# Two cond blocks on one core: layer 1's normalized y transposed in 64-row tiles, two at a time, with every order and bank chosen anew

## The reference

```python
# layer 0 (8 heads of 32)
xn = ln(x); q = softmax(xn@Wq+bq, per head); k = softmax(xn@Wk+bk, over tokens); v = xn@Wv+bv
y  = q @ (k^T v)                                  # per head, 32x32 states
hh = ln(y)*(1+scale)+shift;  x = x + silu(hh) @ W_out + b_out
# layer 1 (16 heads of 16)
xn = ln(x); att = softmax(q k^T over m);  y = att @ v
h  = ln(y)*(1+scale)+shift;  x = x + silu(h) @ out_w + out_b
```

## Time and profile before

| | |
|---|---|
| median of 3 runs | 822.89 us (822.42 to 824.58) |
| profiled execution: span | 824.9 us, 27262 instructions |
| mean granted TensorE clock | 0.989 |
| busy: PE, DVE, ACT, POOL | 797.7, 735.6, 704.5, 688.7 us |
| PE matrix products | 9407 |

### The profile page before, as it was taken

One profiled execution on the slowest core, in us unless ns is written; L12 is line 12 of the kernel. 1 busy time (PEld: TensorE's weight loads), 2 busy tenths in 40 slices (PEclk: granted clock), 3 DMA queues, 4 the chain that ended last, 5 costly groups with the idle time before them and its releaser, 6 DMA issues.

```text
span 824.9 us, 27262 instructions
## 1 busy us (share of the span) xinstructions
PE 797.7 (97%) x9407; PEld 572.0 (69%) x9407; DVE 735.6 (89%) x1488; ACT 704.5 (85%) x1658; POOL 688.7 (83%) x1021
## 2 busy tenths in 40 slices
PE   7998999999999999999999999999999999999995
PEld 3575776777777777677777777777777777666643
DVE  6899999998989999989898889989898989898962
ACT  2366678999898998898898998889989999999995
POOL 8579899999878999789898999888889987896423
PEclk9899999999999999999999999999999999999998
DMA  7522355354344443334545543353454433444411
GB/s 184 153 40 67 96 140 133 81 119 112 86 108 109 105 126 102 98 90 98 122 107 136 121 98 84 84 134 106 110 122 109 109 88 80 99 104 128 116 34 39
DMA packets 149276, 86.11 MB, mean 104 GB/s; under 512 B 87404, under 2 KB 141802, under 8 KB 149130
## 3 DMA queue, kind: packets, MB, share of 16 engines
q1 hardware_dynamic: 149140, 84.36, 42.4%
HBM read 39.64 MB, written 25.80 MB: 79 GB/s over the span
## 4 chain that ended last, share of the span: by engine, by line
PE 41%; issue 12%; POOL 9%; DVE 9%; DMA 2%; SPq 1%; ACT 1%; POOLq 0%; DVEq 0%; ACTq 0%
PE banks L708 11%; PE banks L861 7%; PE banks L716 5%; PE banks L835 4%; PE banks L848 4%; PE banks L723 3%; DVE NM L1308 3%; PE banks L738 2%; PE banks L787 2%; PE banks L871 2%; DVE st L1199 1%; POOL YN L2015 1%; POOL rs L2011 1%; POOL ZHL L2036 1%; POOL SH L2088 1%
## 5 line engine op out<-in xcount | busy, mean ns | idle before, releaser
L1308 DVE TENSOR_REDUCE NM<-banks 128x4 f32<-128x1024 f32 x256 | 306.4, 1212 | 25.1 <-PE banks L835 24.0
L1807 ACT ACTIVATE wraw<-banks 128x1024 f32<-128x1024 f32 x154 | 155.9, 1034 | 8.0 <-PE banks L848 7.3
L2011 POOL TENSOR_TENSOR rs<-ve,nhalf 128x2 f32<-128x2 f32 x128 | 89.7, 703 | 31.6 <-ACT ve L1682 31.4
L1807 ACT ACTIVATE PX<-banks 128x1024 f32<-128x1024 f32 x102 | 103.5, 1035 | 8.6 <-PE banks L848 7.3
L2088 POOL TENSOR_TENSOR SH<-ST,SH 128x512 f16<-128x512 f32 x64 | 74.4, 1164 | 31.4 <-ACT SH L1771 31.4
L708 PE MATMUL banks<-wo,SH 128*128 128x256 f16 x768 | 94.9, 274 | 4.5 <-POOL SH L2088 4.4
L708 PE MATMUL banks<-wv,ZT 128*128 128x256 f16 x768 | 93.5, 273 | 1.4 <-DVE wv L1404 0.5
L835 PE MATMUL banks<-SK,SQ 51*128 51x256 f16 x1024 | 92.5, 272 | 0.8 <-ACT wemb L1815 0.3
L848 PE MATMUL banks<-SQ,SK 53*128 53x256 f16 x1024 | 90.6, 271 | 2.1 <-DVE NM L1308 1.0
L2036 POOL TENSOR_TENSOR ZHL<-Z,ZHL 128x256 f16<-128x256 f32 x128 | 87.5, 704 | 2.6
L861 PE MATMUL banks<-wraw,V 128*32 128x256 f32 x1232 | 87.2, 385 | 0.8 <-DVE NM L1308 0.8
(11 more groups left out here) (186 smaller groups left out, 1879.5 us busy)
## 6 DMA issues: line engine op xcount, KB each, us to landing
scr<-AB SPq DMA_DIRECT2D x64, 256.0 KB, 2.6
X<-in_x_dram SPq DMA_DIRECT2D x32, 256.0 KB, 2.8
SK<-scr SPq DMA_DIRECT2D x64, 128.0 KB, 2.9
SQ<-scr SPq DMA_DIRECT2D x64, 128.0 KB, 2.7
out_dram<-wemb SPq DMA_DIRECT2D x32, 256.0 KB, 2.5
SK<-scr SPq DMA_DIRECT2D x64, 64.0 KB, 2.9
SQ<-scr SPq DMA_DIRECT2D x64, 64.0 KB, 2.7
wemb<-in_L_cond_W_emb_dram SPq DMA_DIRECT2D x1, 1024.0 KB, 5.5
```

What stands on the lines that cost most here:

```text
L1308: V.tensor_reduce(NMe[:, c, :, 2 * g:2 * g + 2], banks[:, n:n + 2, :].rearrange("p a (h m) -> p a h m", m=T), AX.X, ALU.max, negate=True). ...
L1807: A.activation(px(v % 5), banks[:, n:n + 2, :].rearrange("p a n -> p (a n)"), ACT.Exp, scale=r_uu).then_inc(S["exp"])
L2011: G.tensor_tensor(rs[:, b % 2, l, :], ve[:, b % 2, l, :], nhalf[:, :], ALU.pow).then_inc(S[f"r{l}"])
```

## The change

`y1T` is no longer 4 transposes of 128 rows into one bank but 8 of 64 rows: each 128x128 block is turned as its lower and its upper 64 tokens, the lower into bank n and the upper into bank n+1, so that the two lie in different halves of the array. The moving operand, a piece of the identity, has 64 columns in place of 128, the stationary one 64x128. `th_of` reads layer 1's result over the two banks in runs of 64 elements and writes TH and HH as before (they stay contiguous). `gy1T` now needs two free banks, its first always 0, 2, 4 or 6.

```diff
+            def half_transposes(n, src):
+                for a in range(2):
+                    for f in range(2):
+                        for h in range(2):
+                            r = slice(HALF * h, HALF * h + HALF)
+                            m = PE.transpose(banks[:, n + h, f * P + a * HALF:f * P + a * HALF + HALF], src[r, a, f * P:(f + 1) * P],
+                                             ident[r, r])
+                return m
...
             def y1T(b):
                 e.wait_ge(S["yn1"], b + 1)
                 clear(e, "gy1T", b)
-                transposes(home("gy1T", b), YN[:, 1]).then_inc(S["y1T"])
+                half_transposes(home("gy1T", b), YN[:, 1]).then_inc(S["y1T"])
...
+            def turned(M, l, k):
+                return M[:, l, k, :].rearrange("p (a h j) -> p a h j", a=2, h=2) if l else M[:, l, k, :]
+
+            def of_turned(l, n, k):
+                if l == 0:
+                    return bank(n)[:, k, :]
+                return banks[:, n:n + 2, k * P:(k + 1) * P].rearrange("p h (a j) -> p a h j", a=2)
...
                 for k in range(2):
-                    A.activation(TH[:, l, k, :], bank(n)[:, k, :], ACT.Tanh, bias=hB[:, l, k, b:b + 1],
+                    A.activation(turned(TH, l, k), of_turned(l, n, k), ACT.Tanh, bias=hB[:, l, k, b:b + 1],
                                  scale=hA[:, l, k, b:b + 1])
                 for k in range(2):
-                    i = A.activation(HH[:, l, k, :], bank(n)[:, k, :], ACT.Identity, bias=fB[:, l, k, b:b + 1],
+                    i = A.activation(turned(HH, l, k), of_turned(l, n, k), ACT.Identity, bias=fB[:, l, k, b:b + 1],
                                      scale=fA[:, l, k, b:b + 1])
...
-    "gy1T": "71477300023554175724706543174653",
+    "gy1T": "22066264220466242404400406466600",
...
     "gy1T": (
-        "max:29 at:10 th0:9 exp:39 exp:47 exp:55 yt:31 exp:71 exp:79 exp:88 exp:95 yt:51 exp:110 max:132 "
+        "exp:16 Y0:9+at:10 max:46 max:53 max:61 exp:55 exp:64 exp:72 max:91 exp:88 max:109 exp:104 max:124 max:131 "
...
```

```diff
-            ld_m(); ld_w0(); x_in(0); x_in(1); ld_r(); ld_o0(); ld_c(); x_in(2); fd(); mbd0(); ld_f0(); z0T(0)
+            ld_m(); x_in(0); ld_w0(); mbd0(); ld_c(); x_in(1); fd(); ld_o0(); ld_r(); am(0); z0T(0); x_in(2); ld_f0()
```

More of the change, by code:

```diff
@@ L49 @@
[L49 to L67, removed]
@@ L91 @@
-    "go1": "77002057550012516235333440150322",
+    "gt_o0": "2",
+    "gbb0": "3",
+    "grow3": "4",
+    "ga_o0": "0",
+    "gcnd": "5",
+    "gbb1": "2",
+    "gk0": "14351504245220412017350771421607",
+    "gq0": "35223303754635105141241226740026",
+    "gfx0": "0",
+    "gkt": "11202545635546425571015676470564",
+    "gv0": "32466043371555444206274751561017",
+    "gqt": "21036120433375627000653471627452",
+    "gfm0": "0",
+    "gat": "10422543136026235740066601443662",
+    "gt_f0": "0",
@@ new lines @@
+    "gy0": "15411335220304445510026303622433",
+    "ga_f0": "0",
+    "gt_w1": "0",
+    "gy0T": "16740040625603506043370057055262",
+    "ga_w1": "0",
+    "gbb2": "1",
+    "go0": "63325724226635250043231133456224",
+    "grw": "3",
+    "gcol": "1",
+    "gt_b": "1",
+    "ga_b": "1",
+    "gfx1": "5",
+    "gk1": "00346633620523611774600256661352",
+    "gfm1": "0",
+    "gt_o1": "4",
+    "gq1": "24447740777543446542202644773223",
+    "gv1": "75275474474666446454757157617531",
+    "gt_f1": "1",
@@ new lines, in _ @@
+            rows(7, 5); pv(5, 6); pv(5, 7); v1p(8); q0(13); rows(7, 6); cols(6, 0); ty(5, 1); v0(13); cols(6, 1)
+            cols(6, 2); ktT(13); o1(4); qtT(12); rows(7, 7); cols(6, 3); cols(6, 4); o0(10); k1p(9); q1p(9)
+            rows(8, 0); pv(6, 0); pv(6, 1); cols(6, 5); rows(8, 1); rows(8, 2); pv(6, 2); pv(6, 3); pv(6, 4); pv(6, 5)
+            cols(6, 6); rows(8, 3); cols(6, 7); y0T(11); v1p(9); y0(12); rows(8, 4); y1T(5); pv(6, 6); att(13)
+            pv(6, 7); k0(14); cols(7, 0); rows(8, 5); qtT(13); q0(14); ty(6, 0); ty(6, 1); cols(7, 1); rows(8, 6)
@@ new lines, in _ @@
+            o1(5); ktT(14); k1p(10); o0(11); cols(7, 2); rows(8, 7); cols(7, 3); q1p(10); v0(14); cols(7, 4)
+            rows(9, 0); cols(7, 5); pv(7, 0); pv(7, 1); pv(7, 2); pv(7, 3); cols(7, 6); rows(9, 1); rows(9, 2)
+            pv(7, 4); pv(7, 5); rows(9, 3); cols(7, 7); y0(13); rows(9, 4); y1T(6); pv(7, 6); pv(7, 7); att(14)
+            ty(7, 0); y0T(12); k0(15); rows(9, 5); cols(8, 0); ty(7, 1); q0(15); v1p(10); cols(8, 1); cols(8, 2)
+            rows(9, 6); o1(6); v0(15); cols(8, 3); cols(8, 4); rows(9, 7); k1p(11); ktT(15); o0(12); qtT(14); q1p(11)
@@ new lines, in _ @@
+            cols(14, 5); rows(16, 1); pv(14, 0); pv(14, 1); pv(14, 2); pv(14, 3); rows(16, 2); cols(14, 6)
+            rows(16, 3); pv(14, 4); pv(14, 5); y1T(13); cols(14, 7); y0(20); ktT(21); ty(14, 0); y0T(19); v0(22)
+            k0(22); rows(16, 4); pv(14, 6); pv(14, 7); cols(15, 0); rows(16, 5); cols(15, 1); q0(22); cols(15, 2)
+            rows(16, 6); ty(14, 1); k1p(18); v1p(17); ktT(22); cols(15, 3); rows(16, 7); cols(15, 4); q1p(18); o1(13)
+            qtT(21); o0(19); rows(17, 0); cols(15, 5); rows(17, 1); pv(15, 0); pv(15, 1); att(21); pv(15, 2)
@@ new lines, in _ @@
+            o0(24); qtT(26); ktT(27); rows(22, 0); cols(20, 4); rows(22, 1); q1p(23); v1p(22); cols(20, 5)
+            rows(22, 2); pv(20, 0); pv(20, 1); pv(20, 2); pv(20, 3); rows(22, 3); rows(22, 4); cols(20, 6); y0(26)
+            y1T(19); rows(22, 5); y0T(25); ty(20, 0); k0(28); pv(20, 4); pv(20, 5); rows(22, 6); cols(20, 7)
+            cols(21, 0); q0(28); att(27); pv(20, 6); pv(20, 7); rows(22, 7); cols(21, 1); q1p(24); ty(20, 1); v0(28)
+            k1p(24); o1(19); cols(21, 2); rows(23, 0); cols(21, 3); v1p(23); ktT(28); qtT(27); o0(25); cols(21, 4)
@@ new lines, in _ @@
+            cols(21, 5); rows(23, 1); pv(21, 0); pv(21, 1); pv(21, 2); cols(21, 6); rows(23, 2); cols(21, 7)
+            pv(21, 3); pv(21, 4); pv(21, 5); att(28); rows(23, 3); rows(23, 4); y1T(20); y0(27); v0(29); pv(21, 6)
+            pv(21, 7); cols(22, 0); rows(23, 5); rows(23, 6); ty(21, 0); y0T(26); k0(29); qtT(28); cols(22, 1)
+            rows(23, 7); q0(29); ty(21, 1); v1p(24); o1(20); cols(22, 2); cols(22, 3); o0(26); cols(22, 4)
+            rows(24, 0); ktT(29); k1p(25); q1p(25); rows(24, 1); rows(24, 2); cols(22, 5); pv(22, 0); pv(22, 1)
@@ new lines, in _ @@
+            y0T(29); ty(24, 0); rows(26, 6); rows(26, 7); v1p(27); cols(25, 0); qtT(31); ty(24, 1); cols(25, 1)
+            cols(25, 2); k1p(28); o1(23); q1p(28); rows(27, 0); rows(27, 1); cols(25, 3); o0(29); pv(25, 0)
+            cols(25, 4); rows(27, 2); cols(25, 5); pv(25, 1); pv(25, 2); cols(25, 6); rows(27, 3); pv(25, 3)
+            pv(25, 4); pv(25, 5); cols(25, 7); rows(27, 4); y1T(24); y0(31); rows(27, 5); ty(25, 0); y0T(30)
+            pv(25, 6); pv(25, 7); rows(27, 6); cols(26, 0); v1p(28); ty(25, 1); cols(26, 1); rows(27, 7); cols(26, 2)
@@ new lines, in _ @@
+            pv(28, 7); cols(29, 0); cols(29, 1); rows(30, 7); ty(28, 1); v1p(31); cols(29, 2); cols(29, 3); o1(27)
+            cols(29, 4); rows(31, 0); pv(29, 0); pv(29, 1); rows(31, 1); rows(31, 2); cols(29, 5); pv(29, 2)
+            pv(29, 3); cols(29, 6); rows(31, 3); pv(29, 4); cols(29, 7); rows(31, 4); pv(29, 5); y1T(28); rows(31, 5)
+            rows(31, 6); pv(29, 6); pv(29, 7); cols(30, 0); cols(30, 1); rows(31, 7); ty(29, 0); cols(30, 2)
+            ty(29, 1); cols(30, 3); cols(30, 4); pv(30, 0); cols(30, 5); pv(30, 1); cols(30, 6); cols(30, 7)
@@ L1186, in _ @@
+            pv(30, 2); pv(30, 3); pv(30, 4); pv(30, 5); y1T(29); pv(30, 6); pv(30, 7); ty(30, 0); ty(30, 1)
+            cols(31, 0); cols(31, 1); o1(28); cols(31, 2); cols(31, 3); pv(31, 0); pv(31, 1); cols(31, 4); pv(31, 2)
+            cols(31, 5); pv(31, 3); cols(31, 6); pv(31, 4); cols(31, 7); pv(31, 5); pv(31, 6); pv(31, 7); ty(31, 0)
+            ty(31, 1); y1T(30); o1(29); y1T(31); o1(30); o1(31)
         @block.vector
```

922 lines of the change are left out of this document (428 added, 494 removed), and 167 rows, old and new, of the table FREED.

## The result

The changed kernel takes 831.53 us in the median of four runs (829.95 to 832.55), the kernel before 823.2 us beside it (822.42 to 824.58): a ratio of 1.0091 with a 95% interval of 1.007 to 1.0112. It is slower by 0.9%, where 818 us were forecast; the time lies outside the range.

What follows compares the result with a forecast made beforehand. PE's list was taken to set the time. Saving 5.8 us at y1T less 0.8 for shape changes gave -5.0 on a profiled 824.9: 819.9, or 818 us for the median, range 812 to 827.

Steps and rivals of the forecast that it cites:

- What bounds the kernel: From 120 to 780 us PE sets the time, free for only 5.8 of 660 us; time saved there shortens the whole.
- y1T as it is and as it becomes: On PE, a y1T piece falls from 0.436 to 0.245 us, all 32 from 16.0 to 10.2: 5.8 us saved.
- The third rival: y1T's eight weight loads go one after another on PE, 0.49 us a piece: 825.7 us; chance 0.11.
- What the new order costs on PE: Array shape changes rise from 512 to 516, with more on the way out of other pieces: +0.8 us.
- Around it: ACT's two-bank reading, the second bank (0 to 9.6 us) and the reordered set-up were all priced at nothing.
- The fourth: Rival: every y1T waits for its second bank, 0.3 us a time: 827.5 us; chance 0.06.
- The first rival: Gain hidden: PE's waits for maxima, exponentials or the bank pair grow by what is saved: 822.5 us; chance 0.22.
- The second: Rival: the five new lists matter more than the piece, saving some 5 us more at start and end: 813; chance 0.12.
- What would show it: Signs to check in the new profile: for right, pairs 0.06 us apart and loads together; for wrong, marks of the rivals.

Runs made afterwards that it cites:

- e7: Changed kernel's lists and new tile, but the kernel before's order up to 130 us and bank numbers searched anew behind it; 1.0001 of the kernel before.
- e6: Changed kernel with only the bank numbers after the set-up searched anew over its own trace; 1.0029 of the kernel before.
- e12: Changed kernel with its bank numbers searched a second time, over the trace of e6; 1.0033 of the kernel before.
- e4: Kernel before's lists and old tile, with e3's banks and a second bank kept for nothing at y1T; 833.71 us, 1.0091 of the kernel before.
- e5: Kernel before with only the bank numbers after the set-up searched anew; 0.9979 of the kernel before.
- e2: Changed kernel's lists and bank numbers with the old tile in one bank, without the wait for a second bank; 1.0133 of the kernel before.
- e1: Changed kernel's lists, banks and waits with the old tile, the second bank still waited for and kept; 836.88 us, 1.0123 of the kernel before.
- e15: Lists, banks and waits of e7 with the old tile, the second bank still kept; 1.006 of the kernel before.
- e3: Kernel before's lists with the new tile in two banks, bank numbers searched over the kernel before's trace; 835.36 us, 1.0111 of the kernel before.
- e10: Kernel before's lists with the new tile, bank numbers searched again over the trace of e3; 1.0096 of the kernel before.

## Why the prediction was wrong

**What bounds the kernel.** Read rightly as to the engine, wrongly as to its slack. I took PE's 5.8 free us in 660 for all that it waits. From start to start the pieces of that stretch were delayed by 12.9 us already (9.4 and 3.5 in the table), of which the prediction counted less than half. A product's modelled end lies some 270 ns behind its start, while the next may start after 110, so the first 160 ns of a delay are covered by the record of the piece before and count as busy.

**y1T as it is and as it becomes.** Right. In the same shape 0.244 for the 0.245 forecast, entered 0.299 (0.301), left 0.339 (0.341). Float32 loads in two halves do go side by side, which no row of before showed; 0.060 a pair for 0.061. The third rival (serial loads) falls. The Trainium skill ("TensorEngine Tiling (Array Packing)", Key Properties) says that different tiles can load weights and multiply in parallel. This trace agrees for float32 loads: eight in 0.35 us.

**What the new order costs on PE.** Right: work 716.9 to 712.1, -4.8 us for the forecast -5.0, changes of shape included.

**Around it: the failed step.** "I take nothing" was said of three things. ACT's reading over two banks did cost nothing. "PE's 3.0 and 3.7 free us up to 90 us can shrink or grow by as much, and I take nothing": the new order up to 130 us costs 2.3 to 2.6 us (e7 against e6 and e12). And the second bank: "between 0 and 32 x 0.3 = 9.6 us; I take nothing, because each `y1T` already waited for one bank without being listed". The place was wrong: the delays ahead of `y1T` with its banks just freed come to 0.4 us in the changed kernel's steady stretch and to 2.5 at most in any run with the old lists. The price in the old lists is 9 us (e4 against e5), close to the upper bound of 9.6. The new lists escape it (e2 is no faster than e1), but have bank numbers that cost 5 us (e6) and more delay of their own: e6 and e7 stand at 33.7 and 33.8 us of delay where the old lists with banks from the same search have 25.5 (e5).

By ratios, before at 1: the tile -0.006 (e15 against e7, with the changes of shape that it saves), the set-up +0.003, the bank numbers +0.006, which makes +0.003; what is left to 1.0091, 0.006 or 5 us, is with the lists. That term is e15 itself, 1.006: the new main lists with before's set-up, searched banks and the old tile. Each of these terms is a difference of two ratios and uncertain by 0.003 or so. A part of what is with the lists is work, 719.0 us in e15 for 716.9, and a part is the delay at `cols`(b, 0) by the transfer `SQ<-ntd`, 0.6 us in e15 and 2.8 in e7, which the old lists don't have. That the rest is there because room had to be made for a second bank is argued: e3, e4 and e10 show that in the old lists there is too little of it, but not that no better lists exist.

**The rivals.** The fourth named the resource and the sign, and gave 827.5; it charged the wait to `y1T`, with 1.5% of the bank time as the case against. That share was the wrong measure. Banks in use from 120 to 780 us: 5.7 of 8 on average in both kernels, all eight 14% of the time before. What counts is whether one more is free in the 3 us of each `y1T`. In the kernel before all eight were in use at some time of those 3 us at 23 of the 32 `y1T`; in e2, the new lists with one bank for `y1T`, at none. So the new lists did make the room that they were made for. The first rival's mechanism, PE's waits growing by what is saved, is what the profiles of e3 and e4 show (work 3.3 us less, delays 2.9 more); in the lists of e7 and e15 the gain came through. The second had the size of the lists' effect right, some 5 us and more, and the sign wrong. I gave slower 0.15; "five lists are new" should have been weighed as a cost as well as a chance, since no row showed that the new ones were as good.

**What would show it.** "DVE's and ACT's names growing in PE's waits" pointed to rivals 1 and 4, and they did grow: in the two rows for ACT `cols` waited 5.0 us before and 6.6 after, and for DVE 5.4 and 7.8. "PE free for about 6 us of a steady stretch that is 5 us shorter" failed in both halves.

## What to carry to other kernels

Measure slack on a pipelined engine from start to start, against the fastest of the same kind; its busy share hides every wait shorter than the modelled tail. When an edit takes one more buffer, don't price it by its share of buffer time or at the piece that takes it: go through the trace and ask at each use whether one more was free until it is given back (here it was not at 23 of 32), and look for the wait in the pieces behind it too. When a change brings new orders with it, run the new lists with the old instruction and the old lists with the new one: here the instruction was worth -5 us and the rest of the change +13. And compare early windows of two profiles only where their granted clocks agree.

## What the runs showed of the hardware

Of the pieces delayed by over 60 ns with their bank just freed, more than half in the changed kernel and in e3 start their first product 0.145 us after the reader's instruction ends (`k0`(31) in e3: 685.77 after 685.62), and others 0.06 after it (`cols`(26, 5)). The two 64-row halves run float32 transposes of 64 columns at 0.060 us a pair with all their loads, and a change of shape into such a piece costs 0.055, out of it 0.095. With the old set-up the first score came between 88.0 and 89.6 us in the profiles with a clock of 1.00 from 60 to 90 us, and between 91.3 and 92.4 in those with 0.94; the kernel before itself had medians of 823.2 to 827.3 us on the chips of these runs, so differences under 0.3% rest on the ratios alone.
